# Two graph-attention and mixture-of-experts layers on one core: gathers paced by TensorE, five banks for the first products, one-hots in pairs

## What is computed

```python
Wh = layernorm(x) @ W                    # attention; layer 1 also has the leaky slope 0.2
e = (Wh @ a1)[:, :, None] + (Wh @ a2)[:, None, :]
x = x + elu(softmax(where(adj > 0, e, NEG_BIG)) @ Wh)
top2 = top_k(layernorm(x) @ router, 2)   # 8 experts, hidden 256 (layer 0) or 512 (layer 1)
x = x + tokens + sum(gate * expert(layernorm(x)))   # "+ tokens" in layer 0 only
```

## Time and profile before

| | us |
|---|---|
| three timed runs | 1438.54, 1439.29, 1426.94 |
| their median | 1438.54 |
| the profiled execution's own time | 1430.36 |
| its span | 1428.6 |
| mean granted TensorE clock | 0.856 |

### The profile page before, as it was taken

How to read it: one execution, slowest core, us unless ns; L and a number is a source line. 1 busy time by engine, 2 the same in 40 slices (tenths; PEclk the granted TensorE clock), 3 DMA queues, 4 the chain that set the end, 5 groups by cost and what they waited for, 6 DMA issues and landing times.

```text
span 1428.6 us, 31605 instructions
## 1 busy us (share of the span) xinstructions
PE 1123.7 (79%) x9392; PEld 910.2 (64%) x9393; DVE 964.8 (68%) x1844; ACT 551.0 (39%) x1229; POOL 705.0 (49%) x752
## 2 busy tenths in 40 slices
PE   5988765669999991577667487769999997889995
PEld 4766554348888871355455373549889885668884
DVE  3888688937777762458887797827767664556663
ACT  2646475712222221566766484012222221212221
POOL 3565864045555527756670280045433115677762
PEclk9999855559999995788998658579999998989998
DMA  9211133025555544235452553447766624344430
GB/s 279 55 45 38 60 124 112 1 63 163 162 162 160 165 119 129 85 83 145 123 150 61 147 177 118 3 133 216 201 178 193 147 91 126 111 132 127 124 112 12
DMA packets 126095, 172.53 MB, mean 121 GB/s; under 512 B 35109, under 2 KB 94000, under 8 KB 125744
## 3 DMA queue, kind: packets, MB, share of 16 engines
q0 software_dynamic: 28288, 83.03, 21.9%
q1 hardware_dynamic: 89504, 88.22, 20.0%
q10 hardware_dynamic: 8208, 0.07, 1.0%
HBM read 100.87 MB, written 71.44 MB: 121 GB/s over the span
## 4 chain that ended last, share of the span: by engine, by line
PE 55%; issue 19%; DVE 11%; POOL 6%; ACT 3%; another core or an unknown queue 3%; DMA 2%; DVEq 1%; POOLq 0%; SPq 0%; ACTq 0%
PE bank L926 19%; PE bank L940 19%; PE bank L743 4%; PE bank L909 4%; PE bank L890 3%; DVE X L1240 2%; PE bank L771 2%; POOL arena L628 2%; DVE stats L1230 1%; ACT b_bc L997 1%; PE bank L750 1%; DMA X<-first_rows,gather_row 1%; PE bank L751 1%; DVE X L1321 1%
## 5 line engine op out<-in xcount | busy, mean ns | idle before, releaser
L1149 ACT ACTIVATE arena<-bank,b1T 128x256 f32<-128x256 f32 (+1 forms) x464 | 176.2, 458 | 562.9 <-PE bank L926 363.2
L926 PE MATMUL bank<-arena,WREG 128*128 128x256 f16 (+1 forms) x2784 | 326.5, 270 | 28.2 <-issue 16.6
L940 PE MATMUL bank<-WREG,arena 128*128 x2544 | 304.9, 275 | 21.2 <-issue 13.9
L926 PEld LDWEIGHTS bank<-arena,WREG 128*128 x2784 | 253.8, 99 | 70.7 <-issue 40.4
L940 PEld LDWEIGHTS bank<-WREG,arena 128*128 128x128 f16 x2544 | 246.9, 99 | 61.1 <-issue 29.6
L1644 DVE CAST arena<-arena 128x1024 f16<-128x1024 f32 (+1 forms) x140 | 82.3, 588 | 187.2 <-ACT arena L1149 145.9
L640 POOL DMA_INDIRECT arena<-split_tokens,gather_row x136 | 129.9, 955 | 152.3 <-PE bank L909 64.4
L743 PE MATMUL bank<-wg_sb,arena 128*128 128x258 f32 x512 | 141.6, 423 | 57.6 <-issue 19.7
L576 POOL DMA_INDIRECT WREG<-expert_outputs,pos_both x128 | 126.6, 989 | 91.2 <-issue 35.5
L650 POOL DMA_INDIRECT X<-token_rows,gather_row x72 | 72.5, 1006 | 180.5 <-DMA first_rows<-X 95.9
L743 PEld LDWEIGHTS bank<-wg_sb,arena 128*128 128x128 f32 x512 | 102.4, 209 | 82.4 <-issue 42.6
(11 more groups left out here) (205 smaller groups left out, 1577.4 us busy)
## 6 DMA issues: line engine op xcount, KB each, us to landing
first_rows<-X SPq DMA_DIRECT2D x72, 257.0 KB
expert_outputs<-arena SPq DMA_DIRECT2D x68, 256.0 KB
X<-in_x SPq DMA_DIRECT2D x16, 512.0 KB
split_tokens<-arena SPq DMA_DIRECT2D x16, 512.0 KB, 2.9
stage_w<-in_L_ffn_W SPq DMA_DIRECT2D x16, 512.0 KB
token_rows<-X SPq DMA_DIRECT2D x8, 1024.0 KB
token_rows<-arena SPq DMA_DIRECT2D x16, 512.0 KB, 3.8
stage_w<-in_L_ffn_w SPq DMA_DIRECT2D x16, 256.0 KB, 2.7
```

Of the source, the lines that this page charges most:

```text
L926: last = mm(hb, w1_at(L, ea, wh, kc, fc), tT[:, tb:tb + width], start=n == 0, stop=n == 3 * KC - 1)
L940: last = mm(ob[a], hsrc[:, h0:h0 + P], w2_at(L, e[a % len(e)], wh, fc), start=fc == 0 and n == 0, stop=fc == FC - 1 and n == 2)
L1149: ins = A(hid[:, h0:h0 + width], bank[2 + 2 * (u % 2) + fc // 2][:, b0:b0 + width], ACT.Gelu if L == 0 else ACT.Relu, bias=cut(b1T, ea * F ...
```

## The change

1. The first five product tiles of a layer go to banks 2, 3, 5, 6, 7; tiles 5 to 7 and all later ones use 2 and 3 by turns and wait for the last user of their bank.
2. In layer 0 the third pair's transposes stay ahead of the second pair's product, and ScalarE copies all four pairs before it scales. In layer 1 the product comes first, and ScalarE scales tiles 0 to 3 between the copies and the second squares.
3. In layer 1 the first group's root is worked out in two halves, the first between the two halves of the additions.
4. In layer 1 `add_relu` 0 moves between the two halves of `add_outputs(g + 2)`.
5. One-hots lie as (pair of pairs, number, 2), so TensorE's stride is 2 elements; the tables hold each number twice instead of 16 times.
6. Gathers of slots 3 to 7 of a layer wait for `hidden` of slot s - 3 on TensorE. At the change of phases the gathers of slots R+5 and R+1 wait for output(R+1), the next two pairs for output(R+2) and output(R+3).

```diff
+FIRST_BANKS = (2, 3, 5, 6, 7)
+        def hot(a, n):
+            return a[:, 0:n * BATCH].rearrange("p (c l t) -> p c l t", c=BATCH // 2, t=2)
+        def bank_of(t):
+            return FIRST_BANKS[t] if t < len(FIRST_BANKS) else 2 + t % 2
+        def bank_free(t):
+            return max((u + 1 for u in range(t) if bank_of(u) == bank_of(t)), default=0)
...
-                        nc.gpsimd.iota(t_.rearrange("p (l t) -> p l t", t=BATCH), pattern=[[1, n], [0, BATCH]], base=0, channel_multiplier=0,
+                        nc.gpsimd.iota(t_.rearrange("p (l t) -> p l t", t=2), pattern=[[1, n], [0, 2]], base=0, channel_multiplier=0,
...
+                def first_products(L, s):
+                    if 3 <= s < RING:
+                        pool.wait_ge(h_mm[L], at(s - 2))
...
+                    if u % ST == 0:
+                        first_products(0, t // ST)
...
+                    first_products(1, s)
...
                     for s in range(R, R + EARLY):
+                        if s > R:
+                            pool.wait_ge(o_mm[1], at(s + 1))
                         fetch(s + EARLY)
                         fetch(s)
...
-                    pe.wait_ge(Wh_ev[L], at(t - 1))
+                    if bank_free(t):
+                        pe.wait_ge(Wh_ev[L], at(bank_free(t)))
...
                 project(L, 0, 0)
-                turn_x(L, 0, 2)
+                if L == 0:
+                    turn_x(L, 0, 2)
                 project(L, 0, 1)
+                if L == 1:
+                    turn_x(L, 0, 2)
                 turn_x(L, 0, 3)
...
-                        last = mm(bank[2][:, f * nt:f * nt + wide], lane_hot[g % 2].rearrange("p (l t) -> p t l", t=BATCH)[:, b, :],
-                                  block_hot[g % 2][:, 0:wide * BATCH].rearrange("p (l t) -> p t l", t=BATCH)[:, b, :],
+                        last = mm(bank[2][:, f * nt:f * nt + wide], hot(lane_hot[g % 2], P)[:, b // 2, :, b % 2],
+                                  hot(block_hot[g % 2], wide)[:, b // 2, :, b % 2],
...
                 copy_xT(L, 0, 1)
                 if L == 1:
+                    for j in range(4):
+                        scale_rows(L, 0, j)
                     squares(0, 1)
-                scale_rows(L, 0, 0)
-                scale_rows(L, 0, 1)
                 copy_xT(L, 0, 2)
-                scale_rows(L, 0, 2)
-                scale_rows(L, 0, 3)
                 copy_xT(L, 0, 3)
-                for j in range(4, GT):
+                for j in range(4 * L, GT):
                     scale_rows(L, 0, j)
...
                             add_outputs(g, h)
+                            if g == 0:
+                                first_rstd(4 * h, 4)
...
-                            for h in range(2):
-                                add_outputs(g + 2, h)
+                            add_outputs(g + 2, 0)
                         add_relu(L, g, 0)
+                        if ahead:
+                            add_outputs(g + 2, 1)
                         add_relu(L, g, 1)
...
+                    def numbers(a, first, n):
+                        return a[:, 2 * first:2 * (first + n)].rearrange("p (one l t) -> p one l t", one=1, t=2).to_broadcast([P, BATCH // 2, n, 2])
+                    def per_pair(a, n):
+                        return a.rearrange("p (c one t) -> p c one t", one=1, t=2).to_broadcast([P, BATCH // 2, n, 2])
...
-                    here = ch.mark(tt(lanes_g, lanes.rearrange("p (l t) -> p l t", t=BATCH), rows(lane_of[:, now], P), ALU.is_equal))
+                    here = ch.mark(tt(lanes_g, numbers(lanes, 0, P), per_pair(lane_of[:, now], P), ALU.is_equal))
```

More of the change, by code:

```diff
@@ L179, in build @@
         assert used[0] <= tables_at
-        lanes, blocks = carve(P * BATCH // 2, tables_at).bitcast(BF16), carve(max(STILES) * BATCH // 2).bitcast(BF16)
+        lanes, blocks = carve(P, tables_at).bitcast(BF16), carve(max(STILES)).bitcast(BF16)
         lane_hot = [carve(P * BATCH // 2, 0 if h == 0 else None).bitcast(BF16) for h in range(2)]
@@ L739, in project @@
                     t = GT * n + 2 * q + a
-                    pe.wait_ge(Wh_ev[L], at(t - 1))
+                    if bank_free(t):
+                        pe.wait_ge(Wh_ev[L], at(bank_free(t)))
                     for c in range(KC):
                         b = (q % 2) * 512 + (2 * a + c) * P
-                        last = mm(bank[2 + t % 2][:, 0:WA], xT[:, b:b + P], wg(L, c, 0, WA), start=c == 0, stop=c == KC - 1)
+                        last = mm(Wh_bank(t), xT[:, b:b + P], wg(L, c, 0, WA), start=c == 0, stop=c == KC - 1)
                     last.then_inc(Wh_mm[L], 1)
@@ L977, in scale_rows @@
                 if j == 0:
-                    act.wait_ge((rstd_ready if L else pool_rstd)[L], at(n + 1))
+                    act.wait_ge((rstd_ready if L else pool_rstd)[L], at(n + 1 + (L == 1 and n > 0)))
                     act.wait_ge(H_mm[L], at(4 * n - 4))
+                if L == 1 and t == 4:
+                    act.wait_ge(rstd_ready[1], at(2))
                 act.wait_ge(Wh_mm[L], at(t + 1))
-                A(Wh[n % 2][:, j * WA:(j + 1) * WA], bank[2 + t % 2][:, 0:WA], ACT.Identity,
+                A(Wh[n % 2][:, j * WA:(j + 1) * WA], Wh_bank(t), ACT.Identity,
                   scale=one("rstd", t), bias=minus_one[:]).then_inc(Wh_ev[L], 1)
@@ L1271, in first_norm, with first_rstd @@
                 ts(r.bitcast(I32), v.bitcast(I32), -0.5, float(ROOT_GUESS), ALU.mult, ALU.add).then_inc(var_ready[0], 1)
-            def first_rstd(g):
-                v, r_, u = (one(n, g * GT, GT) for n in ("var", "rstd", "ta"))
-                dve.wait_ge(squares_done[1], at(2 * g + 2))
+            def first_rstd(first, n):
+                v, r_, u = (one(c, first, n) for c in ("var", "rstd", "ta"))
+                dve.wait_ge(squares_done[1], at((first + n) // 4))
                 ch.mark(ts(v, v, 1.0 / D, EPS, ALU.mult, ALU.add))
@@ L1355, in _ @@
                     if L == 1 and g + 1 < GROUPS:
-                        first_rstd(g + 1)
+                        first_rstd((g + 1) * GT, GT)
                     if g:
@@ L1574, in _ @@
+                    def per_pair(a, n):
+                        return a.rearrange("p (c one t) -> p c one t", one=1, t=2).to_broadcast([P, BATCH // 2, n, 2])
                     if g >= 2:
                         dve.wait_ge(inv_mm[L], at(g - 1))
-                    here = ch.mark(tt(lanes_g, lanes.rearrange("p (l t) -> p l t", t=BATCH), rows(lane_of[:, now], P), ALU.is_equal))
-                    ch.mark(tt(blocks_g, blocks[:, f * nt * BATCH:(f + 1) * nt * BATCH].rearrange("p (l t) -> p l t", t=BATCH), rows(block_of[:, now], nt), ALU.is_equal))
+                    here = ch.mark(tt(lanes_g, numbers(lanes, 0, P), per_pair(lane_of[:, now], P), ALU.is_equal))
@@ L1578, in _ @@
+                    ch.mark(tt(blocks_g, numbers(blocks, f * nt, nt), per_pair(block_of[:, now], nt), ALU.is_equal))
+                    codes_g = per_pair(row_code[:, now].bitcast(BF16), nt)
                     if L == 0:
                         ch.wait(here)
-                        tt(lanes_g, lanes_g, rows(row_code[:, now].bitcast(BF16), P), ALU.mult).then_inc(hot_ready[L], 1)
+                        tt(lanes_g, lanes_g, per_pair(row_code[:, now].bitcast(BF16), P), ALU.mult).then_inc(hot_ready[L], 1)
@@ L1581, in _ @@
                     elif f == 0:
                         ch.wait()
-                        tt(blocks_g, blocks_g, rows(row_code[:, now].bitcast(BF16), nt), ALU.mult).then_inc(hot_ready[L], 1)
+                        tt(blocks_g, blocks_g, codes_g, ALU.mult).then_inc(hot_ready[L], 1)
                     else:
                         ch.wait()
-                        places_g = block_hot[g % 2][:, nt * BATCH:2 * nt * BATCH].rearrange("p (l t) -> p l t", t=BATCH)
+                        places_g = hot(block_hot[g % 2], wide)[:, :, nt:2 * nt, :]
@@ L1587, in _ @@
                         first_place = place_code[:, g * BATCH - TILES:(g + 1) * BATCH - TILES]
-                        ch.mark(tt(places_g, blocks_g, rows(first_place.bitcast(BF16), nt), ALU.mult))
+                        ch.mark(tt(places_g, blocks_g, per_pair(first_place.bitcast(BF16), nt), ALU.mult))
                         ch.wait()
-                        tt(blocks_g, blocks_g, rows(row_code[:, now].bitcast(BF16), nt), ALU.mult).then_inc(hot_ready[L], 1)
+                        tt(blocks_g, blocks_g, codes_g, ALU.mult).then_inc(hot_ready[L], 1)
```

9 lines of the change are left out of this document (5 added, 4 removed).

## The result

| us | before | changed |
|---|---|---|
| median of the runs (4 each) | 1438.14 | 1416.02 |
| the profiled execution, its span | 1430.36, 1428.6 | 1410.09, 1408.3 |

A forecast was written before the change was run, and what follows sets the result against it. No engine was full; waits counted, with "issue" stalls read as instructions late behind dense gathers. Terms summed to -37.9 us: 1392.5 against the profiled execution, 1400.5 against the median, so 1396 us was forecast, range 1376 to 1421.

The forecast's parts named there:

- 1, 2 and 4b: Layer 0's five first banks -3.0 us; one-hots -4.7 in layer 0, -3.7 in layer 1; layer 1's relu between halves -8.
- 3, the first look-ahead: Experts' start: gathers of slots 3 to 7 wait for hidden products; -2.5 us in layer 0, -5 in layer 1.
- the copies could start sooner: Experts' starts: layer 0's copies 1.9 and 3.6 us sooner; layer 1's at 943.5 instead of 948.50.
- late slots 5 to 7: Layer 0's experts: paced slots come 0.8 us too late, paid about twice, 1.5 us.
- 4, layer 1's start: Layer 1's attention start: root in halves brings the first softmax 8 to 9 us sooner, some given back; -7 us.
- ScalarE scales tiles 0 to 3 at about 559: Layer 1's attention start: scaling at about 559 instead of 573.5, so products of tiles 2 to 6 need no wait.
- the second half ends at about 572 as now: Layer 1's attention start: the root's second half ends at about 572, but only tiles 4 to 7 hang on it.
- 5, change of phases: Layer 1's change of phases: pacing the gathers ends the stall sooner; a third of 11.5 us, -4.
- one stall under 8 us: Sign at the change of phases: products every 5.7 us with a single stall under 8 us.
- A: Rival: stalls at experts' starts and phase change come from the code, the pace frees nothing; about 1412 us, chance 0.22.
- B: Rival: layer 1's attention gains are given back, parts 4 and 4b sum to -6 instead of -15; 1405 us, chance 0.2.
- C: Rival: VectorE drops to one element a cycle in the one-hots, +21.6 and +15.4 us; 1441 us, chance 0.08.

The follow-up runs named there:

- experiment 10: The kernel before with one edit, layer 1's first relu between the two halves of the additions; ratio 0.9944 to the kernel before, groups 187.1 us.
- experiment 4: The changed kernel without the waits of slots 3 to 7 for hidden products; ratio 0.9865 to the kernel before.
- experiment 2: The changed kernel with layer 1's second sixteen attention gathers held until ScalarE has scaled its fourth tile; ratio 0.9859 to the kernel before.
- experiment 1: The changed kernel with layer 1's root undivided and ScalarE's second squares ahead of its first four scalings again; ratio 0.9793 to the kernel before, median 1410.6.

## Why the forecast gain was twice the real one

- **1, 2 and 4b, banks, one-hots, relu: right.** -3.8, -4.8, -3.8 and -8.4 against -3.0, -4.7, -3.7 and -8. Each was read from one wait that an engine really had for another. For the relu the price of the edit alone agrees (experiment 10, 8 us); for the banks and one-hots there is only the stage table.
- **3, the first look-ahead: wrong.** The step that failed is "the copies could start sooner", taken for a gain to the end. They do (14.6 instead of 20.3 us, 17.7 instead of 26.1), but I counted only the gathers of slots 3 to 7 and never asked what the ring's older rule lets loose behind slot 7. It releases the same gathers in one run, and the stalls come there: 0 instead of -7.5 in experiment 4, and over all profiles a loss of some 4 us in layer 1. The late slots 5 to 7, for which I allowed 1.5 us, cost about 0.8.
- **4, layer 1's start: wrong, by 12 us.** The step that failed is "ScalarE scales tiles 0 to 3 at about 559". That is 21 us after the stage's first gather (538.01 before, 530.90 after); tile 0 was scaled after 20.3 us, but tiles 1 to 3 after 30.7, 41.2 and 44.7. I took VectorE's chain for the place of the stall, since the trace of before shows it there, and moved work out of its way into the same stream of gathers; but the stall goes with the stream, not with the chain. It held up two of ScalarE's scalings by 10 us each, and with the squares queued behind them the second root was ready 49.4 us after the first gather (580.3), not 34. I had written that "the second half ends at about 572 as now", which presumed an undisturbed ScalarE.
- **5, change of phases: right in size.** -4 forecast, -2 to -5 by kernels on the same chip, -7.4 in the one profile. The sign that I had given for it, one stall under 8 us, did not come: there are three, of 13.7, 12.2 and 10.4.
- **The rivals.** A gave 1412, nearest to the 1416 measured, by a mechanism that experiment 2 refutes: the stalls do not come from the code. Its consequence, that part 3 frees nothing, holds for another reason. That its sum is near is luck: it had -4 for layer 1's start, which measured +5.0, and 0 for the phase change, which measured -7.4. What I lacked was the third case, that the stall is real, is due to the gathers, and merely moves. The Trainium skill ("Runtime: NRT & Kernel Launch", section "Instruction fetch mechanics") calls the fetching of instructions mostly hidden. Experiment 2 shows that the gathers cost time all the same (10 us between two scalings with them, 2 without), but not that they do it by late instructions, so no run here decides on that page. B did not happen: the groups kept their 8.4 us. C did not: L1616 takes 1.23 us, so runs of two cost VectorE nothing. The Trainium skill ("Vector Engine (DVE) Microarchitecture Reference", section "5.1 Performance modes — why throughput varies by op and dtype") agrees.
- **What stays open.** Why the medians give experiment 1 some 9 us and its profile 3; what it is about a run of gathers that stops other engines, and whether it stops their instructions; and why not every run does it. In the changed kernel nine runs of eight gathers, 629.6 to 738.8 us, leave no engine an "issue" or "remote" wait over 2.2 us.

## What to carry to other kernels

Where several engines stall on "issue" or "remote" beside a long run of indirect gathers, suspect the run before the code: before holding it back, follow GpSimd's queue to where it catches up, and price the code that will stand there. Let it catch up slowly where a slot leaves GpSimd time (layer 1's first phase: two gathers, 2.5 us, in a slot of 5.7), and leave it alone where it doesn't (layer 0: 2.5 of 3.1 us). And put no short chain of one engine behind another in such a run; a gain read from a true wait between two engines is far safer than one read from a stall.

## What the runs showed that I had not expected

- A starved TensorE often starts one matmul every 0.7 or 1.4 us, in transposes (597.49 to 599.62 in experiment 2) as in output products (963.81 to 965.96 in the changed kernel); ScalarE's long stalls are of 4 to 12 us.
- Halving the gathers' bytes left two of ScalarE's stalls at 9.87 and 9.92 us.
- Two IOTAs of 2,048 and 2,304 elements took 5.20 us, of 256 and 272 still 3.18: I had them down as nearly nothing, and the next gathers starting 4.5 us sooner; they started 45.0 us after the stage's first instead of 45.9 (583.91 and 575.92).
